# A fused attention and ternary feed-forward kernel: the first two tiles' work written out per engine, and the first batch's x turned by TensorE

## What is computed

```python
x = x + attention(layernorm(x), ctx, mask)      # softmax(x ctx^T / sqrt(512)) ctx, masked
y = layernorm(x)
a, b = linear(y, w1, g1), linear(y, w2, g2)     # 512 -> 2048
x = x + linear(silu(a) * b, w3, g3)             # 2048 -> 512

def linear(x, w, g):
    xq = act_quant(g * x * rsqrt(mean(x * x) + 1e-8))      # rows to 8 bits, scale 127 / max|x|
    s = mean(abs(w))                                       # one number for the whole matrix
    wq = round(tanh(w / (s + 1e-8))) * arctanh(s)          # ternary weights
    return xq @ wq.T
```

## Time and profile before

| | before |
|---|---|
| median of 3 runs | 456.91 us |
| profiled execution | 456.24 us, its span 454.4 us |
| busy TensorE, VectorE, ScalarE, POOL | 396.6 (87%), 400.7 (88%), 342.7 (75%), 342.7 (75%) us |
| mean granted TensorE clock | 0.944 |
| chain that ended last | TensorE 54%, VectorE 16%, ScalarE 10%, issue 10%, DMA 3%, POOL 3% |
| DMA | 67.44 MB, mean 148 GB/s; over 400 GB/s in many slices before 45 us |

### The profile page before, as it was taken

How to read it: one execution, slowest core, us unless ns; L and a number is a source line. 1 busy time by engine, 2 the same in 40 slices (tenths; PEclk the granted TensorE clock), 3 DMA queues, 4 the chain that set the end, 5 groups by cost and what they waited for, 6 DMA issues and landing times.

```text
span 454.4 us, 8236 instructions
## 1 busy us (share of the span) xinstructions
PE 396.6 (87%) x1854; PEld 176.2 (39%) x1854; DVE 400.7 (88%) x927; ACT 342.7 (75%) x615; POOL 342.7 (75%) x539
## 2 busy tenths in 40 slices
PE   7226553799999999999999999999999999999994
PEld 6002221244444444344434444444344444444442
DVE  3799776789999999999999999999999999999863
ACT  1586545987898879986998699878988796777752
POOL 0168758788878888788878887888778887888860
PEclk9655695999999999999999999999999999999999
DMA  6999821444668436734674467644684425454531
GB/s 265 396 375 412 292 103 23 126 107 100 92 180 198 92 95 173 191 86 115 184 170 96 115 117 206 151 99 109 167 191 92 101 63 114 90 109 95 128 70 46
DMA packets 110503, 67.44 MB, mean 148 GB/s; under 512 B 100752, under 2 KB 100880, under 8 KB 106768
## 3 DMA queue, kind: packets, MB, share of 16 engines
q1 hardware_dynamic: 110480, 67.19, 56.6%
HBM read 34.14 MB, written 8.39 MB: 94 GB/s over the span
## 4 chain that ended last, share of the span: by engine, by line
PE 54%; DVE 16%; ACT 10%; issue 10%; DMA 3%; POOL 3%; SPq 1%; DVEq 1%; POOLq 0%; ACTq 0%
PE S L1180 33%; PE DN L1209 16%; DVE stageB L920 4%; DVE hm L926 4%; DMA X<-in_w1T 3%; PE R L1159 3%; ACT stageB L695 2%; ACT L650 2%; ACT prob L650 2%; ACT sg L703 2%; DVE X L960 1%; POOL W2q L574 1%; ACT junk_x L673 1%; PE R L1134 1%; ACT W1q L724 1%
## 5 line engine op out<-in xcount | busy, mean ns | idle before, releaser
L525 POOL TENSOR_TENSOR stageB<-stageB,g3b 128x512 f32<-128x512 f32 x128 | 163.8, 1287 | 34.1 <-DVE stageB L920 28.8
L1180 PE MATMUL S<-W2q,q12T 128*128 128x512 f16 x512 | 134.8, 387 | 3.0 <-DVE W2q L995 2.6
L1180 PE MATMUL S<-W1q,q12T 128*128 128x512 f16 x512 | 135.1, 388 | 0.3 <-ACT sg L703 0.2
L1209 PE MATMUL DN<-W3q,stageB 128*128 128x512 f16 x512 | 125.7, 379 | 3.9 <-DMA stageB<-stageB 3.1
L703 ACT ACTIVATE sg<-S,asc 128x512 f32<-128x512 f32 x128 | 86.8, 681 | 24.3 <-PE S L1180 19.8
L920 DVE TENSOR_TENSOR stageB<-sg,S 128x512 f32<-128x512 f32 x128 | 85.7, 676 | 16.9 <-ACT sg L703 10.5
L926 DVE TENSOR_REDUCE hm<-stageB 128x1 f32<-128x512 f32 x128 | 86.2, 675 | 0.2 <-POOL stageB L525 0.2
L695 ACT ACTIVATE stageB<-stageB,hf 128x1024 f16<-128x1024 f32 x64 | 69.9, 1141 | 8.9 <-DVE hf L946 8.9
L1180 PEld LDWEIGHTS S<-W2q,q12T 128*128 128x128 f16 x512 | 50.0, 99 | 68.0 <-DVE W2q L995 4.0
L1180 PEld LDWEIGHTS S<-W1q,q12T 128*128 128x128 f16 x512 | 48.9, 99 | 67.7 <-ACT sg L703 10.3
L1209 PEld LDWEIGHTS DN<-W3q,stageB 128*128 128x128 f16 x512 | 49.0, 98 | 64.9 <-DMA stageB<-stageB 4.1
(11 more groups left out here) (115 smaller groups left out, 424.2 us busy)
## 6 DMA issues: line engine op xcount, KB each, us to landing
xTs<-in_xT SPq DMA_DIRECT2D x8, 1024.0 KB, 6.9
X<-in_x SPq DMA_DIRECT2D x8, 1024.0 KB, 6.2
out_x<-X SPq DMA_DIRECT2D x32, 256.0 KB, 2.7
X<-in_w1T SPq DMA_DIRECT2D x4, 1024.0 KB, 12.5
stageB<-in_w2T SPq DMA_DIRECT2D x4, 1024.0 KB, 20.5
X<-in_w3T SPq DMA_DIRECT2D x4, 1024.0 KB, 9.3
ctxr<-in_ctx SPq DMA_DIRECT2D x16, 128.0 KB, 3.0
ctxc<-in_ctx SPq DMA_DIRECT2D x8, 128.0 KB, 4.0
```

The costliest lines, as they stand in the source:

```text
L525: nc.gpsimd.tensor_tensor(gh[q][:, part], hp[:, part], g3b[:, part], ALU.mult).then_inc(s_gh_made, 1)
L1180: mm = nc.tensor.matmul(bank[n % 2][:, :], q12T[q][:, i * KD + k, :], w[:, n, k, :], start=(k == 0), stop=(k == KD - 1))
L1209: mm = nc.tensor.matmul(DN[:, :], q3T[:, k, :], W3q[:, k, :], start=(k == 0), stop=(k == KH - 1))
```

## The change

The first two slots are taken out of slot(b, j), which loses its flag first; batches starts at slot(0, 2). What slots 0 and 1 did is appended to each engine's opening list, call by call, in an order of its own. The load of xT for batch 0 is gone: TensorE turns x from SBUF into the four PSUM banks that up uses later (turn_x, 16 transposes of 128x128), and ScalarE copies them to xTs (x_turned, four copies of 128x512). The scores of batch 0 wait for these copies one at a time. Beside it the arctanh series has two terms fewer, arctanh_choice is two operations in place of four, W2 part 1 is scaled by ScalarE in place of POOL (POOL now scales one part of W2, and quantize_3(0, 0) waits for one), W1 part 3 is scaled behind silu(0, 0), stage_a_mean has one wait more, and the loads and DMA transposes of the first two slots stand in SyncE's list between the weight loads. The code from slot 2 on has only the flag's conditions removed. Cut to its core:

```diff
@@ -163,6 +163,7 @@
+xP = S1 + S2
...
-    four(0, first=True, attn=True, prep=True)
+    for j in range(2, TPB):
+        slot(0, j, attn=True, prep=True)
...
     load_ctxc(0)
-    load_xT(0)
     load_x(0)
     for k in range(WC):
...
+    load_ctxc(1)
     transpose_12(0, 0)
-    load_ctxc(1)
-    load_xT(1)
     sp.dma_start(g3b[:, :], g3.partition_broadcast(P)).then_inc(s_gain3_in, 16)
     sp.wait_ge(s_w1_act, 1)
     load_w(stageA, w3T, 0, w_in[2][0])
+    load_ctxr(1)
     sp.wait_ge(s_w1_act, 2)
     load_w(stageA, w3T, 1, w_in[2][1])
+    load_xT(1)
+    transpose_12(1, 1)
+    sp.wait_ge(s_w1_pool, 1)
+    load_w(stageA, w3T, 2, w_in[2][2])
     load_x(1)
-    load_ctxr(1)
-
+    sp.wait_ge(s_w1_act, 3)
+    load_w(stageA, w3T, 3, w_in[2][3])
+    load_x(2)
+    load_ctxc(2)
+    transpose_12(2, 0)
+    for h in range(NHALF):
+        transpose_3(0, h)
+    load_xT(2)
+    sp.wait_ge(s_w3_act, 2)
+    sp.wait_ge(s_w3_dve, 1)
+    sp.wait_ge(s_w3_pool, 1)
...
@@ -464,6 +468,7 @@
         pool.wait_ge(s_x1_made, t + 1)
         if later(t):
             pool.wait_ge(s_a_ga, 2 * t)
+            pool.wait_ge(s_a_vs, t)
         pool.nop(nofuse=True)
         nc.gpsimd.tensor_scalar(anm[:, :], x1sum[:, j:j + 1], -1.0 / D, 0.0, ALU.mult, ALU.add).then_inc(s_a_nm, 1)
...
+        elif n == 0:
+            pool.wait_ge(s_w2_act, t + 1)
...
-        step(nc.gpsimd.tensor_scalar(r, sq, 1.0 / 17, 1.0 / 15, ALU.mult, ALU.add))
-        for k in range(13, 0, -2):
+        step(nc.gpsimd.tensor_scalar(r, sq, 1.0 / 13, 1.0 / 11, ALU.mult, ALU.add))
+        for k in range(9, 0, -2):
             step(nc.gpsimd.tensor_scalar(r, r, sq, 1.0 / k, ALU.mult, ALU.add))
...
-        step(nc.gpsimd.tensor_tensor(high[:, cols], high[:, cols], lns[:, 0, cols], ALU.mult))
-        step(nc.gpsimd.tensor_tensor(r, r, high[:, cols], ALU.add))
-        nc.gpsimd.tensor_scalar(wc[:, cols], r, 1.0 / (QMAX * QUANTUM), 0.0, ALU.mult, ALU.add).then_inc(s_coef_ready, 1)
+        nc.gpsimd.tensor_scalar(wc[:, cols], lns[:, 0, cols], high[:, cols], r, ALU.mult, ALU.add).then_inc(s_coef_ready, 1)
...
     attention(0)
     stage_a_mean(0, 0)
     stage_a_root(0)
+    stage_a_mean(1, 1)
+    quantize_12(0)
+    arctanh_series(0)
     weight_scale(0, stageA, W1f, 2, s_w1_pool)
-    quantize_12(0)
-    stage_a_mean(1, 1)
-    arctanh_series(0)
     stage_a_root(1)
-    weight_scale(1, stageB[:, :], W2f, 1, s_w2_pool)
     arctanh_choice(0, 1)
     stage_a_worth_gate(0)
     weight_scale(1, stageB[:, :], W2f, 3, s_w2_pool)
+    stage_a_mean(2, 2)
+    quantize_12(1)
+    arctanh_series(1)
+    stage_a_mean(3, 3)
+    stage_a_worth_gate(1)
+    pool.wait_ge(s_gain3_in, 16)
+    gain_3(0, 0, 0)
+    stage_a_root(2)
+    gain_3(0, 1, 0)
+    gain_3(0, 2, 0)
+    quantize_12(2)
+    gain_3(0, 3, 0)
+    arctanh_choice(1, 1)
+    stage_a_worth_value(0)
+    stage_a_root(3)
+    attention(1)
+    stage_a_worth_value(1)
+    gain_3(1, 0, 1)
+    gain_3(1, 1, 1)
+    stage_a_worth(2, 2)
+    stage_h_root(0, 0)
+    arctanh_series(2)
+    arctanh_choice(2, 2)
+    weight_scale(2, stageA, W3f, 2, s_w3_pool)
+    gain_3(1, 2, 1)
...
+    def x_turned(k):
+        act.wait_ge(s_turn_x, k + 1)
+        nc.scalar.copy(xTs[:, k, :, :].rearrange("p j q -> p (j q)"), xP[k][:, :]).then_inc(s_xT_turned, 1)
...
     table(0, ACT.Exp)
     attention_ccT(0)
+    for k in range(KD):
+        x_turned(k)
     attention_half(0)
     weight_abs(0, stageA, 0, s_w1_abs)
     attention_exp(0)
@@ -741,25 +758,51 @@
     weight_abs(0, stageA, 2, s_w1_abs)
     stage_a_var(0)
     weight_abs(0, stageA, 3, s_w1_abs, WN // 2)
-    for k in (0, 1, 3):
-        weight_scale(0, stageA, W1f, k, s_w1_act)
-    stage_a_var(1)
+    weight_scale(0, stageA, W1f, 0, s_w1_act)
+    weight_scale(0, stageA, W1f, 1, s_w1_act)
     weight_abs(1, stageB[:, :], 2, s_w2_abs)
     weight_abs(1, stageB[:, :], 3, s_w2_abs, WN // 2)
+    stage_a_var(1)
     table(1, ACT.Ln)
     logs(0, 2, 1)
+    weight_scale(1, stageB[:, :], W2f, 1, s_w2_act)
     table(2, ACT.Silu)
     weight_scale(1, stageB[:, :], W2f, 2, s_w2_act)
-
+    silu(0, 0, 0)
+    weight_scale(0, stageA, W1f, 3, s_w1_act)
+    silu(0, 1, 0)
+    stage_a_var(2)
+    weight_abs(2, stageA, 0, s_w3_abs)
+    silu(0, 2, 0)
+    weight_abs(2, stageA, 1, s_w3_abs)
+    attention_ccT(1)
+    silu(0, 3, 0)
+    square(0, 0)
+    silu(1, 0, 1)
+    stage_a_var(3)
+    weight_abs(2, stageA, 3, s_w3_abs)
+    silu(1, 1, 1)
+    attention_half(1)
+    square(0, 1)
+    silu(1, 2, 1)
+    weight_scale(2, stageA, W3f, 0, s_w3_act)
+    silu(1, 3, 1)
+    attention_exp(1)
+    weight_scale(2, stageA, W3f, 3, s_w3_act)
+    attention_probT(1)
+    quantize_3(0, 0, 0)
+    logs(2, 3, 2)
+    square(1, 0)
+    quantize_3(0, 1, 0)
+    table(3, ACT.Silu)
...
     stage_a_gain(0)
     weight_abs(0, stageA, 3, s_w1_abs, WN // 2)
+    weight_mean(0, WC + 1)
     stage_a_max(0)
-    weight_mean(0, WC + 1)
+    weight_abs(1, stageB[:, :], 0, s_w2_abs)
     stage_a_factor(0, 0)
+    weight_clip(W1f, 0, s_w1_act, 1, s_w1_q)
     attention_x1(0, 1)
-    weight_abs(1, stageB[:, :], 0, s_w2_abs)
-    weight_clip(W1f, 0, s_w1_act, 1, s_w1_q)
     weight_abs(1, stageB[:, :], 1, s_w2_abs)
-    weight_clip(W1f, 1, s_w1_act, 2, s_w1_q)
     weight_abs(1, stageB[:, :], 3, s_w2_abs, WN // 2)
+    stage_a_gain(1)
     weight_mean(1, WC + 1)
     weight_scale(1, stageB[:, :], W2f, 0, s_w2_dve)
+    stage_a_max(1)
     weight_clip(W2f, 0, s_w2_dve, 1, s_w2_q)
+    stage_a_factor(1, 1)
+    weight_clip(W1f, 1, s_w1_act, 2, s_w1_q)
+    weight_clip(W2f, 1, s_w2_act, 1, s_w2_q)
     weight_clip(W1f, 2, s_w1_pool, 1, s_w1_q)
+    weight_clip(W2f, 2, s_w2_act, 2, s_w2_q)
+    gate(0, 0)
+    stage_a_gain(2)
     weight_clip(W1f, 3, s_w1_act, 3, s_w1_q)
-    stage_a_gain(1)
-    weight_clip(W2f, 1, s_w2_pool, 1, s_w2_q)
-    stage_a_max(1)
-
+    stage_a_max(2)
+    attention_cc(1)
+    weight_clip(W2f, 3, s_w2_pool, 1, s_w2_q)
+    gate(0, 1)
+    stage_a_factor(2, 2)
+    gate(0, 2)
+    max_3(0, 0, 0)
+    gate(0, 3)
+    weight_abs(2, stageA, 2, s_w3_abs)
+    attention_xstat(1)
+    gate(1, 0)
+    weight_mean(2, WC)
+    max_3(0, 1, 0)
+    gate(1, 1)
+    attention_softmax(1)
+    max_3(0, 2, 0)
+    gate(1, 2)
+    max_3(0, 3, 0)
+    weight_clip(W3f, 0, s_w3_act, 1, s_w3_q)
+    stage_h_top(0)
+    gate(1, 3)
+    stage_h_factor(0, 0, 0)
+    stage_a_gain(3)
+    attention_norm(1)
+    stage_a_max(3)
+    weight_scale(2, stageA, W3f, 1, s_w3_dve)
+    attention_x1(1, 0)
+    max_3(1, 0, 1)
+    stage_a_factor(3, 3)
+    weight_clip(W3f, 1, s_w3_dve, 1, s_w3_q)
+    max_3(1, 1, 1)
+    weight_clip(W3f, 2, s_w3_pool, 1, s_w3_q)
+    max_3(1, 2, 1)
+    weight_clip(W3f, 3, s_w3_act, 2, s_w3_q)
+    dve.wait_ge(s_coef_ready, 3)
...
         pe.wait_ge(s_ccT_made, a + 1)
         if later(a):
             pe.wait_ge(s_x1_made, TPB * a)
-        pe.wait_ge(s_xT_in, 16 * (a + 1))
+        if later(a):
+            pe.wait_ge(s_xT_in, 16 * a)
         for k in range(KD):
+            if not later(a):
+                pe.wait_ge(s_xT_turned, k + 1)
             for e in range(2):
                 mm = nc.tensor.matmul(R[1][e * M:(e + 1) * M, 0:TPB // 2 * P], ccT[:, k, :], xTs[:, k, e::2, :],
                                       start=(k == 0), stop=(k == KD - 1), tile_position=(0, e * M))
         mm.then_inc(s_half_ps, 1)
+
+    def turn_x():
+        pe.wait_ge(s_x_in, 16)
+        for k in range(KD):
+            for j in range(TPB):
+                mm = nc.tensor.transpose(xP[k][:, j * P:(j + 1) * P], X[:, j * D + k * P:j * D + (k + 1) * P],
+                                         identf[:, :])
+            mm.then_inc(s_turn_x, 1)
...
     attention_ccT(0)
+    turn_x()
     attention_scores(0)
     attention_turn(0)
     attention_probT(0)
@@ -1223,45 +1270,45 @@
     weight_total(0, s_w1_abs, WC + 1)
     attention_readout(0, 1)
     weight_total(1, s_w2_abs, WC + 1)
-
+    up(0, 0, 0)
+    up(0, 1, 0)
+    up(0, 2, 0)
+    attention_ccT(1)
+    up(0, 3, 0)
+    up(1, 0, 1)
+    up(1, 1, 1)
+    attention_scores(1)
+    weight_total(2, s_w3_abs, WC)
+    up(1, 2, 1)
+    attention_turn(1)
+    up(1, 3, 1)
+    attention_probT(1)
+    attention_readout(1, 0)
+    pe.wait_ge(s_w_totred, 3)
```

171 lines of the change are left out of this document (39 added, 132 removed).

## The result

The changed kernel takes 448.6 us in the median of four runs (447.09 to 450.3), the kernel before 456.9 (455.36 to 456.97). The ratio is 0.983, with a 95% interval of 0.980 to 0.986: 8.3 us gained, where 10.6 were forecast. Medians here and in the table are of the executions in the chip's usual state, which leaves out one of 501 us (turn_alone), one of 1059 (short_series_before) and one of 2309 (long_series).

A forecast was written before the change was run, and what follows sets the result against it. Waits between engines before the third slot were the bound: winv 24.5 + 1.1 + 50.8 + idle 4.0 put gate(2, 0) at 80.4 against 91.0. So 456.24 less 10.6, plus 0.67 for the median, gave 446.3 us, range 442.0 to 451.5.

The forecast's parts named there:

- What bounds it: First weight scale to third slot: 65.10 us held by waits between engines, VectorE idle 14.3; the loop cannot be shortened.
- Head: Start to winv: x at 8.3, turn 2.4 us, exponentials at 14.5, winv at 24.5 against 25.9, 1.4 us gained.
- the head is wrong if the exponentials start after 15.3: Sign against the head: ScalarE's first exponentials, forecast at 14.5 against 15.34 before, starting later than 15.3.
- Idle time of the body: VectorE from winv to gate(2, 0): idle 4.0 us in place of 14.3, with bounds of 0.7 and 9.6.
- Up products, silu and totals: VectorE's waits left before gate(2, 0): up products 2.0 us of 4.8, silu 0.5 of 3.3, totals 1.0 of 1.5.
- POOL* loses that scale, two series steps and two choice steps per matrix: POOL before gate(2, 0): busy 46 of 55.9 us, from 49.9 less 2.0 for the scale and some 2 for steps.
- slower rival: VectorE's clips collide with POOL, 1.67 us each; eleven hits give 464.7 us; sign: busy over 54; chance 0.04.
- Busy time of the body: VectorE from winv to gate(2, 0): same operations in another order, 50.8 us, plus 1.1 for stage_a_max(0).
- SyncE: Load list of the first two slots: W3 part 3 issued about 44.5, in at 54; nothing past due by over 1 us.
- a transfer takes the waits' place: Rival: W3 part 3 or x(1) lands some 9 us late, or the loop gives it back; 455.4 us, chance 0.06.
- The forecast one: Main case: gain of 8 to 13 us, 443.9 to 448.9 us, chance 0.62.
- VectorE is packed: Rival, before gate(2, 0): idle only 0.7 us and winv at 24.0 to 24.5; gain 14.1, 442.8 us; chance 0.12.

The follow-up runs named there:

- turn_alone: The kernel before with only the turn of x in place of the load of xT(0), all orders as before; 455.09 us, ratio 0.998.
- short_series_before: The kernel before with the new, shorter arctanh series and choice on POOL and nothing else; 457.46 us, ratio 1.003.
- long_series: The changed kernel with the old arctanh series and choice (two more terms, four choice steps in place of two); 452.73 us, ratio 0.992.
- experiment 1: The changed kernel with xT of batch 0 loaded again and nothing turned, 450.19 us; the kernel before with the turn alone, 455.09 us.
- experiment 3: POOL's coefficient steps: old series and choice in the changed kernel, 452.73 us; new ones in the kernel before, 457.46; changed kernel with slot 2's root first, 447.50.
- root_first: The changed kernel with slot 2's root and slot 1's gate factor ahead of the arctanh series on POOL; 447.50 us, ratio 0.980.
- holes: The changed kernel with stage_a_max(1) ahead of the scale of W2 part 0 and attention_cc(1)'s statistics ahead of W2 part 1's clip; 447.83 us.
- best4: best3 with ScalarE's copy of probT placed between the W3 scales of parts 2 and 3; 447.13 us, ratio 0.980.
- best2: root_first with W3 part 3 issued earlier by SyncE, hidden slot 0's root earlier on POOL, and W3 part 2 scaled by ScalarE; 445.27 us.
- best3: best2 with the two edits of holes; 445.33 us, ratio 0.976.
- experiment 5: Kernels adding edits on top of root_first: earlier W3 part 3 and hidden slot 0's root, 446.11 us; then best2, 445.27; best3, 445.33; best4, 447.13.

## Why the prediction was right, and where it was off

- *What bounds it* was right: 14.3 us of VectorE's idle time before the third slot, of which 10.6 went. Waits, not work, were removed; nothing in the loop moved.
- *Head.* x there at 8.3: the statistics start at 8.11. The turn was put at 2.4 us and measures 1.97, the lower bound of the estimate (0.12 us each for sixteen); the copies ended at 11.3, forecast 11.5. Exponentials 14.75 for 14.5, winv 24.54 for 24.5. That they agree so well is in part luck. The prediction's walk starts from the arrival of x and has no term for the forty matmuls with ones, whose end varies by 1.5 us (experiment 1). Its sign "the head is wrong if the exponentials start after 15.3" holds for this profile, but in six of the eleven profiles with the turn they start later than that. The Trainium skill ("TensorE: Matmul & The Clock Gate", Part 4: PE-mode transpose) gave 4.4 us for the turn (an estimate from its 275 ns for one, of bf16) and exponentials 1.8 us later; the trace disagrees, with 0.12 us for each of the sixteen. Nor was it so that no row before could decide: the kernel before has runs longer than the two it named, such as this one of eight (f16) at its end:

```profile
445.57 0.61 PE L1190 MATMUL S<-ident,stageB 128*128 128x128 f16 x8 [1.83 <-ACT stageB L695]
```

  The turn ran at a granted clock of 1.00, straight behind the matmuls with ones and the transposes of ctx, at the same granted clock since 2.0; whether transposes alone would have brought it, no run shows.
- *Idle time of the body,* forecast 4.0 us, measured 3.7: the right sum from wrong terms, by luck. Up products, silu and totals, put at 3.5 together, came to nothing; 1.1 us are hand-overs too short for the view of waits; and 2.6 us that stood nowhere in the sum are VectorE's wait for POOL's root of slot 2. The failing step is the one on POOL: "*POOL* loses that scale, two series steps and two choice steps per matrix" and "Were the cover gone these steps would be worth what is removed, nothing more". The prediction compared POOL's busy time with the stretch (46 of 55.9) and did not walk its list between two due times. POOL has no pause over 0.2 us from 34 to 54, and with the old steps in place the path is 2.6 us longer, 1.05 of it waiting (experiment 3). Nor is the length of the list the whole of it. In those 20 us POOL's instructions are longer than the shortest of the same kind in this trace: 3.03 for 1.97 (scale), 2.75 for 1.36 (codes), 2.60 for 1.70 (series), 1.31 for 0.33, 1.04 for 0.19, 0.84 for 0.34, 0.65 for 0.19 and 0.62 for 0.19, 6.6 us together. Four of them end 0.04 to 0.06 us behind a scale or clip of VectorE: 38.42 behind 38.37, 40.17 behind 40.11, 43.15 behind 43.11, 51.22 behind 51.18. Without that ak would have been ready about 6 us earlier (an estimate from these rows), ahead of VectorE, which came to it at 51.77. The slower rival looked at what the contact costs VectorE; what it costs POOL stood nowhere, and no run isolates it. The price of the wait is small all the same: with it gone, root_first has gate(3, 0) 0.85 us nearer.
- *Busy time of the body,* put at 51.9 (50.8 and max(0)'s 1.1), is 53.31. This is the whole of the miss at gate(2, 0), 81.58 for 80.4; the idle time gave 0.3 back. The assumption that failed is "the same set of operations ... 50.8 us". The twelve clips and two scales took 12.5 us before and 15.4 after (sums of their groups by line); other operations gave some back (softmax's last step 1.27 and now 0.79). That is the mechanism of the slower rival, at a small part of its price: one full clip and one scale hit (1.6 and 1.1 us), one W2 clip at 0.4 beside POOL's codes, and three W3 clips at about 0.5 each, the first beside POOL's scale and two beside its gain_3. The rival needed eight hits of 1.67. VectorE's busy time stayed under the 54 that was named as its sign.
- *SyncE.* W3 part 3, forecast to be issued at 44.5, was issued at 48.36, since SyncE stood before transpose_12(1, 1) until 45.95 (POOL's codes ended at 45.87). ScalarE waited 0.7 us for it, which did not show in VectorE's waits; in root_first, where the rest was 3 us earlier, it waited 2.5. The rival "a transfer takes the waits' place" is real, one step behind the wait that still covered it.
- *From gate(2, 0) to the end.* 9.38 us there, 9.02 at gate(3, 0), 8.3 in the median. 0.36 is slot 2's head start on the pattern, which was foreseen. Another 0.55 went between the fourth and the sixth slot, where TensorE stood for the transposed h of slot 1:

```profile
91.87 1.02 PE L1255 MATMUL DN<-W3q,stageB 128*128 128x512 f16 x4 [1.47 <-DMA stageB<-stageB]
```

  It isn't tied to the change: from gate(3, 0) to gate(5, 0) the kernel before takes 24.05 us, seven of the experiments 24.05 to 24.09, short_series_before, long_series and turn_alone 24.16 to 24.36, and the changed kernel, holes and best4 24.60 to 24.62. The profiled execution lost more later on. Between there and the last gate it lost 0.9 us, most of it at the same wait (0.62 us at 413.15), and behind the last gate 1.7. There the last down products took 5.06 us in place of 3.62, at a granted clock of 0.71 in place of 1.00:

```profile
439.63 5.06 PE L1255 MATMUL DN<-W3q,stageB 128*128 128x512 f16 x16
```

```profile
446.98 3.62 PE L1209 MATMUL DN<-W3q,stageB 128*128 128x512 f16 x16
```

  From the last gate to the end, six of the fourteen profiles take 14.40 to 14.47 us (before, turn_alone, long_series, root_first, best2, best3) and the other eight 16.08 to 16.19. So two profiled executions can differ by 1.7 us at the very end without regard to what was changed (before and short_series_before, with the same code there, stand on either side), and differences of medians of that size (root_first, holes, best4) are to be read beside the distances of the table. Why the clock is lower in some, no run shows.
- *Which cases came true.* The forecast one, at its weak end. Of its signs, winv, VectorE's idle time and the loop's period came out; gate(3, 0) stood 12.85 us behind gate(2, 0) for 12.5, and the W3 total came at 62.20 for "near 60". "VectorE is packed" was not reached by this change, but by the kernels of experiment 5 (idle 2.2 to 3.4), and there the other half of the truth shows: a packed VectorE pays for its neighbour.

## What to carry to other kernels

When waits are removed by a hand-written order, walk the list of every engine between two due times, not only its busy share: POOL, 81% busy over the stretch (46.40 of 57.04 us), was without a pause for twenty microseconds just where VectorE needed it. Walk it with the lengths that its small steps have beside VectorE's clips, not with their shortest: at their shortest, by the estimate above, this wait would not have shown. Price work "under cover" by the cover that the new order leaves, not by the old one. And expect removed waits to return as smaller ones on the next engine, and as longer instructions where VectorE and POOL now meet; put reductions and statistics beside POOL's long scales, and clips elsewhere. Last, one profile of a head that jitters by a microsecond does not price half a microsecond in it.

## What was not expected of the hardware

Cutting POOL's 128x2048 scale (1.97 us alone, 3.03 in contact) into four of 128x512 (0.69 each at the shortest) turns the contention round: VectorE's neighbours lose less (the W2 scale takes 1.73 in place of 2.34, the longest W1 or W2 clip 1.10 in place of 2.26), and POOL takes 4.6 to 4.7 us for the same columns. The Trainium skill ("SBUF — State Buffer", SBUF: two separate sides) says that the pair is locked for a whole instruction; the traces agree for long instructions, where VectorE's clip ended 0.55 us after POOL's scale. What they add is that with short ones it is mostly POOL that waits (why, no run here shows), and that even a POOL step of 128x1 can be held until a scale of VectorE has ended: avk took 1.04 us for 0.19. And not every operation of VectorE asks for it: the reduction (1.21 us) and the statistics (0.67) beside POOL's scale took what they take alone.
